# A decoder layer with experts on one core: no normalisation stages of their own, loads, fills and the weight split spread out, and both expert slots joined in front of the down-projection

## The reference, cut to what matters

```
x = x + attn(layernorm(x))                 # x: 64 x 128 x 128, 16 heads of 8, causal, rope
x = x + xattn(layernorm(x), ctx, ctx)      # 77 keys, a temperature per head from a small MLP
x = x + ffn(layernorm(x))
# ffn, for each token: the two best of 8 experts, softmax weights over the two
common_w1, common_w3 = x @ w_gate.T, x @ w_up.T                 # 128 -> 512
d1, d3 = (x A1^T) B1^T * 2, (x A3^T) B3^T * 2                   # low rank 16, for each expert
act = silu(common_w1 + d1) * (common_w3 + d3)
out = (sum_e weight_e act_e) @ w_down.T + sum_e weight_e (act_e A2^T) B2^T * 2
```

## Time and profile before

| | us |
|---|---|
| median of 3 runs (1767.62 to 1772.02) | 1767.89 |
| the profiled execution | 1771.94 |
| its span | 1770.1 |
| first matmul at | 40.79 |
| busy: PE, PEld, DVE, ACT, POOL | 1641.4, 1231.9, 1232.2, 924.0, 880.6 |

### The profile page before, as it was taken

The page is one execution under the profiler, slowest core; times in us unless marked ns, Lnnn a source line. Parts: engine busy times, 40 slices in busy tenths (PEclk is TensorE's granted clock), DMA queues, the critical chain, the costliest instruction groups (busy, mean ns, idle before and its releaser), DMA issues. The chain is left out here.

```text
span 1770.1 us, 42709 instructions
## 1 busy us (share of the span) xinstructions
PE 1641.4 (93%) x14274; PEld 1231.9 (70%) x14336; DVE 1232.2 (70%) x2839; ACT 924.0 (52%) x2183; POOL 880.6 (50%) x977
## 2 busy tenths in 40 slices
PE   0899999999977899999999999995999999999998
PEld 0455555555545666666666666555999999999998
DVE  4577777777755667776767767615787887887876
ACT  1345455445443566665666666644545555454453
POOL 0444444444426676776776767621343343443442
PEclk9999999999996899998999989987999999999999
DMA  6000000000000000000000000000000000000000
GB/s 170 2 2 1 1 1 1 1 1 1 1 7 6 4 7 6 7 7 6 7 7 6 7 6 7 2 2 1 8 8 7 9 6 9 9 6 9 9 6 13
DMA packets 26456, 16.60 MB, mean 9 GB/s; under 512 B 6194, under 2 KB 23667, under 8 KB 26355
## 3 DMA queue, kind: packets, MB, share of 16 engines
q1 hardware_dynamic: 26354, 15.29, 3.1%
HBM read 10.03 MB, written 4.19 MB: 8 GB/s over the span
## 5 line engine op out<-in xcount | busy, mean ns | idle before, releaser
L293 ACT ACTIVATE sa_P<-sa_SK 128x1024 f32<-128x1024 f32 x128 | 131.4, 1027 | 150.8 <-PE sa_SK L438 150.8
L1458 POOL TENSOR_TENSOR ff_zz<-ff_zt 128x256 f32<-128x256 f32 x32 | 38.4, 1199 | 319.4 <-DVE ff_zt L1655 319.4
L250 POOL TENSOR_TENSOR sa_KM<-sa_HQK,sc_headmask 128x512 fp32r<-128x512 f32 x64 | 66.6, 1041 | 245.7 <-ACT sa_HQK L288 245.7
L865 ACT ACTIVATE xa_P<-xa_SK 77x1024 f32<-77x1024 f32 x128 | 130.1, 1017 | 98.0 <-PE xa_SK L1157 97.7
L1526 ACT ACTIVATE ff_SG<-bank 128x512 f32<-128x512 f32 x128 | 76.8, 600 | 192.5 <-PE bank L1728 192.5
L1645 DVE TENSOR_TENSOR ff_GL<-ff_GU,ff_GH 128x512 fp32r<-128x512 f32 x128 | 147.7, 1173 | 27.4 <-ACT ff_GH L1531 27.1
L366 DVE TENSOR_REDUCE sa_mx<-sa_SQ 128x8 f32<-128x1024 f32 x128 | 156.6, 1223 | 11.1 <-PE sa_SQ L438 8.3
L1793 PE MATMUL bank<-fh_r,ff_GH 128*128 128x256 f32 x512 | 148.2, 290 | 0.0
L1726 PE MATMUL bank<-ff_ZH,fh_b 128*128 128x256 f32 x512 | 147.8, 289 | 0.0
L791 POOL TENSOR_TENSOR xa_QMH<-xa_QBH,xc_headmask 128x512 fp32r<-128x512 f32 x64 | 72.8, 1138 | 148.2 <-ACT xa_QBH L855 148.1
L1727 PE MATMUL bank<-ff_ZL,fh_b 128*128 128x256 f32 x512 | 145.1, 283 | 0.0
(11 more groups left out here) (259 smaller groups left out, 5381.2 us busy)
## 6 DMA issues: line engine op xcount, KB each, us to landing
xa_shift<-xa_row SPq DMA_DIRECT2D x256, 2.0 KB
out<-X SPq DMA_DIRECT2D x64, 64.0 KB, 1.5
xa_cx<-ctx SPq DMA_DIRECT2D x64, 38.5 KB
sa_shift<-sa_mT SPq DMA_DIRECT2D x64, 8.0 KB, 1.8
fr_b<-L_ffn_B SPq DMA_DIRECT2D x2, 256.0 KB, 3.9
fr_r<-down_a SPq DMA_DIRECT2D x1, 512.0 KB, 4.7
fr_w<-L_ffn_w_gate SPq DMA_DIRECT2D x1, 256.0 KB, 3.5
fr_w<-L_ffn_w_up SPq DMA_DIRECT2D x1, 256.0 KB, 3.6
```

The lines of the kernel that those rows point to most:

```text
L293: nc.scalar.activation(P[:, 2 * (k % 2) + h, :], SK[:], ACT.Exp).then_inc(p_ready, 1)
L865: nc.scalar.activation(P[0:TC, (2 * b + h) % 4, :], SK[0:TC, :], ACT.Exp).then_inc(p_ready, 1)
```

## The change

**Normalisation.** `inverse_std` is gone. A class `Moments` holds the same chain in three pieces, `variance` and `inverse` (DVE) and `root` (ACT), run for a part of the sequences at a time: 0 to 4, 4 to 16 and 16 to 64 inside self-attention's first steps; 0 to 48 in its last steps and 48 to 64 in cross-attention's first; 0 to 56 in cross-attention's last steps and 56 to 64 in the first of the experts.

**Loads.** x comes in five parts (4, 12, 16, 16, 16 sequences); `ident` and `wqkv` right behind the first part. PE waits for these two, and from step -2 for the others. The constants of the later stages are issued in self-attention's steps 0 to 7, the first context tiles at its end. **Fills:** `shift` and `pick_row` are written in steps -3 and -2; VA and mT of cross-attention one slot at a time. **Weight split:** the raw weights are loaded in cross-attention's step 64 into E1 and E2, and split in steps 66 to 73. Rings of cross-attention shrink (SLOTS 16 to 12, VRING 12 to 11).

**Experts.** The two slots are joined before `down`: silu of slot 1 is multiplied by the ratio of the weights (`scaled`, POOL), `gated` writes G1, and `slot_sum` (DVE) adds it to GU. `down` keeps its weights on the array and has features on the partitions: units 0 and 1 give only the 128 columns of A2 (6 products each), units 2 and 3, now the sum, give A2 and w_down (12 each). `z_parts` (DVE) and `z_sum` (POOL) separate the experts with masks that `output_masks` (POOL) makes, `back_T` turns the result, `residual` applies the first slot's weight.

```
 def slot_inputs(g, p, s):   # POOL; as before, for one slot
+def output_masks(g, p):
+    pool.wait_ge(mask_sb, g + 1)
+    need(pool, zb_done, 2 * (g - 1))
+    nc.gpsimd.tensor_tensor(ME[:, p, 1], M[:, 0, :], M[:, 1, :], ALU.add).then_inc(me_done, 1)
+    pool.wait_ge(me_done, 2 * g + 1)
+    nc.gpsimd.tensor_tensor(ME[:, p, 0], ME[:, p, 1], M[:, 0, :], ALU.subtract).then_inc(me_done, 1)
+def scaled(g, u):
+    pool.wait_ge(rb_sb, g + 1)
+    pool.wait_ge(silu_done, UNITS * g + 2 + u + 1)
+    unit2 = SG[:, u, :].rearrange("f (c n) -> f c n", c=2)
+    nc.gpsimd.tensor_tensor(unit2, unit2, RB[:].unsqueeze(1).to_broadcast([128, 2, NT]),
+                            ALU.mult).then_inc(scaled_done, 1)
+def z_sum(g):
+    pool.wait_ge(zb_done, 2 * g + 2)
+    need(pool, zl_done, g)
+    nc.gpsimd.tensor_tensor(zs[:], zb[:, 1, :], zb[:, 0, :], ALU.subtract).then_inc(zs_done, 1)
 def step(g, p):
-    if real(g - 1):
-        slot_sum(g - 1)
-    if real(g + 1):
-        slot_inputs(g + 1, 1 - p)
+    if real(g + 1):
+        slot_inputs(g + 1, 1 - p, 0)
+    if real(g - 1):
+        z_sum(g - 1)
+    scaled(g, 0)
+    scaled(g, 1)
+    if real(g + 1):
+        slot_inputs(g + 1, 1 - p, 1)
+        output_masks(g + 1, 1 - p)
...
+def ratio_copy(g):   # ACT
+    act.wait_ge(rb_ps, g + 1)
+    need(act, scaled_done, 2 * g)
+    nc.scalar.copy(RB[:], BF[:, NT:2 * NT]).then_inc(rb_sb, 1)
...
+def slot_sum(g, u):   # DVE
+    dve.wait_ge(gu_done, UNITS * g + 2 + u + 1)
+    nc.vector.tensor_tensor(GU[:, u, :], GU[:, u, :], G1[:, u, :], ALU.add).then_inc(sum_done, 1)
+def residual(g):
+    dve.wait_ge(back_ps, g + 1)
+    for n in range(NB):
+        xb = X[:, bass.ds((NB * g + n) * C, C)]
+        nc.vector.scalar_tensor_tensor(xb, OUT[:, NT + n * C:NT + (n + 1) * C], W0[:, bass.ds(NB * g + n, 1)], xb,
+                                       ALU.mult, ALU.add).then_inc(x_done, 1)
 def step(g, p):
     if real(g - 2):
-        residual_z(g - 2)
+        residual(g - 2)
+    odds(g)
...
-    if real(g - 1):
-        slot_z(g - 1, 1 - p)
     g_lo(g, 1)
     if real(g - 1):
-        residual_y(g - 1, 1 - p)
+        z_parts(g - 1, 1 - p)
+        z_lo(g - 1)
     gated(g, 2)
+    slot_sum(g, 0)
     gated(g, 3)
-    if real(g - 1):
-        z_lo(g - 1)
+    slot_sum(g, 1)
     g_lo(g, 2)
     g_lo(g, 3)
...
 def down(g, k):   # PE
...
+    if k == 2:
+        need(pe, x_done, NB * g)
     for c in range(2):
         f = 2 * u + c
+        unit = [t[:, k, c * NT:(c + 1) * NT] for t in GG]
+        at = k // 2 * NT
+        last = three(PZ[:, at:at + NT], [t[:, f, C:2 * C] for t in RD], unit, f == 0, f == 3, skip_group_check=True)
+        if k >= 2:
+            last = three(OUT[:, 0:NT], [t[:, f, 0:C] for t in RD], unit, f == 0, False, skip_group_check=True)
 def step(g, p):
     up(g, 0, p)
-    down(g, -2)
+    down(g - 1, 2)
     if real(g + 1):
         a_products(g + 1, 1 - p)
+    ratios(g)
     up(g, 1, p)
-    down(g, -1)
     if real(g + 1):
         masks(g + 1)
+    down(g - 1, 3)
     up(g, 2, p)
     up(g, 3, p)
-    if real(g - 1):
-        z_T(g - 1)
-    down(g, 0)
     if real(g + 2):
         input_T(g + 2)
-    down(g, 1)
+    down(g, 0)
     if real(g - 1):
         extra(g - 1)
+    down(g, 1)
     if real(g + 2):
         logits(g + 2)
+    if real(g - 1):
+        back_T(g - 1)
```

More of the change, by code:

```diff
@@ L50, in constant_tiles, with load_constant @@
     return tiles, ctx.enter_context(nc.semaphore(tag + "_loaded"))
[L53 to L62, removed]
+def load_constant(sp, tiles, loaded, constants, name, dram):
+    shape, _, source = constants[name]
+    src = dram[source]
+    if name == "w1b":
+        src = src.unsqueeze(0).to_broadcast(shape)
+    if name == "w1c":
+        src = src[2:3].rearrange("a h -> h a")
+    if name == "b3":
+        src = src.to_broadcast(shape)
+    sp.dma_start(tiles[name][:], src).then_inc(loaded, 16)
@@ L65, in row_stats @@
 def row_stats(nc, X, ST, b):
     return nc.vector.bn_stats(ST[:, bass.ts(b, 6)], X[:, bass.ts(b, C)])
[L70 to L127, removed]
@@ L206, in steps @@
         def steps(eng, step):
-            for n in range(-4, 4):
+            for n in range(-4, START):
                 step(n, n % RING, n // RING)
-            with eng.Fori(1, B // RING - 1) as i:
+            with eng.Fori(START // RING, B // RING - 1) as i:
                 for k in range(RING):
@@ L309, in onT_copy, with fill_shift @@
                 nc.scalar.copy(onT[:], R[:, 0:T]).then_inc(onT_sb, 1)
[L311 to L315, removed]
+            def fill_shift(p):
+                act.wait_ge(others_loaded, ALL_OTHERS)
+                nc.scalar.copy(shift[:, p], future[:].unsqueeze(1).to_broadcast([128, H, T])).then_inc(shift_set, 1)
+            ln.root(act, 0, 0, 4)
             def step(n, k, i):
@@ L389, in stats, with gather @@
                 row_stats(nc, X, ST, b).then_inc(rows_done, 1)
-            dve.wait_ge(loaded, ALL_LOADED)
+            def gather(c, first, last):
+                dve.wait_ge(x_loaded[c], 16)
+                for b in range(first, last):
+                    row_stats(nc, X, ST, b).then_inc(gathered, 1)
+            gather(0, 0, 4)
+            dve.wait_ge(gathered, 4)
+            ln.variance(dve, 0, 0, 4)
+            ln.inverse(dve, 0, 0, 4)
             def step(n, k, i):
+                if isinstance(n, int) and n == -3:
+                    dve.wait_ge(rope_loaded, 32)
                 if real(n + 2):
@@ L408, in step @@
                     row_max(n + 2, 0, k % 2)
+                if not isinstance(n, int):
+                    return
+                if n == -3:
+                    gather(1, 4, 16)
+                    dve.wait_ge(gathered, 16)
+                    ln.variance(dve, 1, 4, 16)
+                if n == -1:
+                    ln.inverse(dve, 1, 4, 16)
+                if 0 <= n <= START - 3:
+                    first, last = 16 + 48 * n // (START - 2), 16 + 48 * (n + 1) // (START - 2)
+                    for c in range(2, 5):
+                        lo, hi = max(first, CHUNKS[c][0]), min(last, CHUNKS[c][1])
+                        if lo < hi:
+                            gather(c, lo, hi)
+                if n == START - 3:
+                    dve.wait_ge(gathered, B)
+                    ln.variance(dve, 2, 16, B)
+                if n == START - 1:
+                    ln.inverse(dve, 2, 16, B)
+                if n == B - 1:
+                    dve.wait_ge(rows_done, 48)
+                    ln.variance(dve, 3, 0, 48)
+                if n == B:
+                    ln.inverse(dve, 3, 0, 48)
             steps(dve, step)
@@ L1473, in step, with first @@
                 if real(g + 1):
-                    slot_inputs(g + 1, 1 - p)
-            groups(pool, lambda: slot_inputs(0, 0), step, lambda: slot_sum(G - 1))
+                    slot_inputs(g + 1, 1 - p, 1)
+                    output_masks(g + 1, 1 - p)
+            def first():
+                slot_inputs(0, 0, 0)
+                slot_inputs(0, 0, 1)
+                output_masks(0, 0)
+            groups(pool, first, step, lambda: z_sum(G - 1))
         @block.scalar
@@ L1546, in step @@
                     spread(g + 1)
+                ratio_copy(g)
                 silu(g, 1)
@@ L1660, in residual_y @@
[L1660 to L1666 removed]
+                dve.wait_ge(me_done, 2 * g + 2)
@@ L1844, in end @@
             def end():
-                down(G, -2)
-                down(G, -1)
-                z_T(G - 1)
+                down(G - 1, 2)
+                down(G - 1, 3)
                 extra(G - 1)
+                back_T(G - 1)
             groups(pe, first, step, end)
```

502 lines of the change are left out of this document (311 added, 191 removed).

## The result

The changed kernel takes 1866.26 us (median of 4 runs, 1861.55 to 1867.61), against 1768.88 of the kernel before on the same chip: 1.0543 times as long, with a 95% interval of 1.0519 to 1.0567. The profiled execution has a span of 1863.9 us.

A forecast was written before the change was run, and what follows sets the result against it. PE was taken to bound the experts' stretch; the change gives -34 us in the front and +127 from a round closed by DVE, ACT and POOL, +93 in all: 1861 us, range 1775 to 1905.

The forecast's parts named there:

- The round: Experts: DVE, ACT and POOL wait on one another in seven stretches, 20.9 us a step instead of 16.8, +127 us.
- Stretch 7: End of the expert step, `gated`(2) to the last `g_lo`: 6.6 us, with four DVE waits for POOL (0.4, 0.4, 1.2, 0.5).
- The rule on the shared ports: Experts: a DVE instruction with two SBUF inputs and a POOL instruction reading SBUF block each other; sparing the sums saves 37 us.
- the round without collisions: Rival, experts: the round holds but DVE and POOL do not collide; 18.0 us a step, +37, 1771 us in all.
- upper bound: Experts' round with each wait of stretch 7 doubled: 22.5 us a step, +177 us.
- few collisions: Rival, experts: no or few DVE and POOL collisions, chance 0.17, spread from 1765 to 1815 us; 0.03 counted as faster.
- The front: Attention and the transitions up to the experts: -34 us; a rival took -15 and 1880 us, widening the forecast alone.
- The start: Self-attention: first matmul at 9 instead of 40.79 us, -31.8; given back 5 (prologue), 5 (statistics), 4 (square roots): -18.
- Between the attentions: Change from self- to cross-attention: -5.5 for the gap; with the VA clearing in small pieces and a later table load, -6.
- Before the experts: Gap ahead of the experts: idle PE from 11.13 to 2 us, -9, and -1 at the 1.2 GHz level, together -10.
- The rival of the clock: Experts: PE's new gaps drop its clock to 1.2 GHz in part of each step, +46, 1907 us; chance 0.10.
- The rival of PE: Experts: PE stays the bound at 15.6 us a step, -38, 1696 us; chance 0.13.

The follow-up runs named there:

- e2: The changed kernel with `gated` of units 2 and 3 writing over H3 in PSUM, so the sums read one bank: 1833.0 us, step 19.9.
- e4: The changed kernel with POOL's two masked inputs of the second slot cut to 16 of 256 columns from the third group on: 1822.6 us.
- e10: e9 with one POOL output mask less, two buffers for the mask M, and the order changed on all four engines: 1792.5 us, step 18.6.
- e5: The changed kernel with all nine POOL instructions of the experts' step cut to 16 of 256 columns from the third group on: 1725.6 us.
- e1: The change's front alone, with the experts' stage of the kernel before (its shift made for 56 and 8 sequences): 1728.5 us, step 16.7.
- e11: The kernel of e1 run once more, on the same chip as e9 and e10: 1726.8 us, step 16.7.
- e9: The changed kernel with sums over H3 in PSUM and instructions reordered on PE, DVE, ACT and POOL: 1728.3 us, step 16.45.

## Why the prediction was right, point by point

The forecast was 1861 us and the result 1866, and its steps held nearly singly.

**The round.** The seven stretches, from the timelines above (the ends that don't stand there are starts of the next group's rows in the same views):

| stretch | forecast | measured | from where |
|---|---|---|---|
| 1 residual to gated(0) | 3.1 | 3.23 | 1500.62 to 1503.85 |
| 2 to the picks | 3.15 | 3.15 | to 1507.00 |
| 3 ACT, to gated(1) | 1.4 | 1.42 | to 1508.42 |
| 4 to POOL's ZH | 1.9 | 2.06 | to 1510.48 |
| 5 and 6, ZH to gated(2) | 4.8 | 4.69 | to 1515.17 |
| 7 to the residual | 6.6 | 6.23 | to 1521.40 |

The sum is 20.78 instead of 20.9, with some luck: stretches 1 and 4 were 0.3 too short together, stretches 5 to 7 0.5 too long. Stretch 7 was sized least well, 0.4 too long. From start to start, as the forecast counts, the sums take 0.99 each (1.1 forecast) and the last two `g_lo` 2.83 together (3.0), and `gated` is on its number. The rows' own lengths are 1.07 and 2.90: I had not taken the 0.1 of overlap off them. Over all the steps from the residual at 1228.60 to that at 1834.35 the mean is 605.75/29 = 20.89 us, so 31 steps give (20.89 - 16.80) x 31 = +127, the number forecast; the stage grew by 133.4. Of the 6 us left, 5 are at the end: from the last residual of a full step to the last instruction are 29.5 us (1834.35 to 1863.9), before 24.8 (1745.31 to 1770.1). I had not counted the ends.

**The rule on the shared ports.** The sums wait for POOL's reads, e2 and e4 show it, and the Trainium skill (SBUF — State Buffer, Who interferes with whom) has it right, also in that a DVE instruction with one SBUF operand is spared, which the page says for instructions outside the 2-port perf modes: `gated` stays at 0.69 beside POOL's rows. Of the price the round without collisions gives 18.0: 2.8 of the 4.0 us lost. The rows of the step agree, as an estimate: two sums 0.38 each above 0.69, `z_lo` 1.03 instead of 0.43 (e10's), the last two `g_lo` 2.90 instead of about 1.3, together 2.9. The split was not measured by itself: e5 takes away POOL's own lengths too. For the two sums the forecast named 1.2 us a step and 37 in all, but its own waits of stretch 7 give 0.4 + 0.4 = 0.8; e2 measured 0.9 and 33. Its upper bound has the like slip: the four waits doubled give 23.4 us, not 22.5. And the chance of 0.03 for a faster time with few collisions does not fit that case's own spread, which starts at 1765. None of the three is a term of the 1861.

**The front.** Forecast -34, measured -39.6 in this pair of profiles and -40 in e1's time. The start was undersized: first matmul at 7.20 (9), last statistics 23.5 us sooner (18), since what I expected back was 14 us and came to 10: the first output product of self-attention stands 51.5 us behind the first matmul instead of 45.6, which is the prologue (5.9 for a term of 5), and the steps give back 4.3 more, for two terms of 5 and 4. Between the attentions it is -4.7 to the first transposition, and 4.3 more by the end of cross-attention, where the sum of the earlier trace rows takes 1.44 instead of 3.50; forecast -6. The forecast reads that row wrongly. What stood first in the clearing's way was not the sum but a copy two instructions in front of it on DVE, which reads one SBUF tile; copy, sum and clearing all end at 547.8, so the sum's 3.50 are mostly its wait behind the copy. Timelines of DVE and POOL before:

```profile
543.49 4.34 DVE L935 COPY xa_w3r<-xc_w 64x128 f32<-64x128 f32 x1
...
544.12 3.63 POOL L735 MEMSET xa_VA<- 128x4240 f32 x1
```

The same copy takes 1.24 us beside the small clearings of the changed kernel. So of DVE's instructions with one SBUF tile, `gated` is spared here and this copy is not.

Before the experts it is -7.1 instead of -9: 4.01 us of idle PE where I took 2. These shares are uncertain by some us: the same front reaches the experts at 1168.49 in e1's profile and at 1176.26 in e11's.

**The signs.** Most came: the first matmul before 9 us, the new sums near 1.1, DVE at 14.6 us in a step, PE's waits before `down`(2) and `extra`. Three did not come as said: POOL is busy for 11.5 us in a step and not near 10; PE idles for 4.01 us before the experts, above the 3 named; and `g_lo` takes 1.09 us in the mean and not above 1.3 (before 1.19), since the first two of each step take 0.69 and only the last pair is held.

**The rival of the clock** was right in its event and wrong in its price. The clock is at 1.00 in the middle of the experts' stage before, in e5 and in e9, whose PE has no gaps or short ones, and it falls in the changed kernel: of eight steps in a row five are at 0.98 to 1.00, two at 0.92 and one at 0.78. The steps at 0.92 last 20.76 to 20.83 us, no longer than those at 1.00, since PE works them off in its idle time (busy 17.56 instead of 16.03). Only the one at 0.78 is longer, 21.51. Four of those are 3 us in all, where the rival priced 46.

**The rival of PE.** PE's need was put at 15.6; e9, whose PE is busy for 386.58 of 400 us at 16.45, shows 15.9. With PE truly at 15.6 us this rival's 1696 asked for an order that was not reached. That the weight loads show TensorE's headroom, as the Trainium skill has it (Perfetto Trace Analysis, Identifying the Most-Contended Engine), agrees with e1 (398.97 of 400 us in e1's middle, no faster) and in the changed kernel reads 156 of 200, headroom that the other engines' round left unused.

## What to carry to other kernels

When the bound engine is relieved by moving work to the others, follow one step of the new order through all engines and close the round: here the instructions were affordable (e9) and their order cost 117 us. A combining step that can read its operand from a PSUM bank instead of a second SBUF tile takes DVE out of POOL's way without an instruction more. And a buffer that saves an instruction has to outlive the last reader in the other engines' order, or it is a new wait (e10).

## What was not expected of the hardware

The collision lengthens both sides at once: the sum from 0.69 to 1.07 and ZH from 1.28 to 1.74 in the same moment, so removing it gives time on two engines. The clock falls to 0.78 in every eighth step only (those that begin at 1291.03, 1458.23, 1625.43 and 1792.64), though every step holds the same work in the same order; what sets that is open. And a DVE copy with a single SBUF tile was held for 4.34 us until POOL's clearing ended, so counting a DVE instruction's SBUF operands does not always tell whether POOL can hold it.
